# Expert slots with one and two turns between their stages, four slots' rows transposed together, all three expert weights copied by ScalarE, and the slot row numbers worked out right behind the tables

## The reference

```python
x = x + L0_attn(layernorm(x))      # 16 sequences of 512 tokens, 128 features: time mixing with a scan, then channel mixing
x = x + L0_ffn(layernorm(x))       # 8192 tokens, 16 experts, the best one alone (K = 1)

logits = hidden @ router_w.T                              # [8192, 16]
top_vals, top_idx = top_k(logits, 1)
scores = sigmoid(scatter(top_vals, at top_idx, else -inf))
routed_in = hidden[None] * scores.T[:, :, None]           # a token's row, scaled, in its own expert; zero in the others
gate, up = split(routed_in @ gate_up_proj[e])             # 128 -> 2 x 128
routed_out = (up * silu(gate)) @ down_proj[e]             # 128 -> 128
shared = silu(hidden @ shared_gate.T) * (hidden @ shared_up.T) @ shared_down.T    # 128 -> 512 -> 128, for every token
return shared + sum over experts of routed_out
```

## Time and profile before

| | us |
|---|---|
| median of the runs | 578.75 |
| the profiled execution, its own time | 577.51 |
| its span, first to last instruction | 575.7 |

### The profile page before, as it was taken

The page is one execution under the profiler, slowest core; times in us unless marked ns, Lnnn a source line. Parts: engine busy times, 40 slices in busy tenths (PEclk is TensorE's granted clock), DMA queues, the critical chain, the costliest instruction groups (busy, mean ns, idle before and its releaser), DMA issues.

```text
span 575.7 us, 10804 instructions
## 1 busy us (share of the span) xinstructions
PE 498.0 (86%) x3012; PEld 401.3 (70%) x3012; DVE 386.0 (67%) x1075; ACT 325.9 (57%) x619; POOL 353.1 (61%) x548
## 2 busy tenths in 40 slices
PE   1778999999999999999999999996698888888730
PEld 0346777877868877878768777995488777777730
DVE  3769999989999799988999797363132233322213
ACT  3666886767876776857776753421154445535410
POOL 5445478768778578867878466447026565565560
PEclk9888999999999999999999999997699999999965
DMA  6005101101101011101011011106423443344207
GB/s 201 1 1 209 49 1 56 57 1 57 38 19 55 12 47 56 37 21 56 10 47 38 2 38 37 38 29 156 112 83 111 112 119 112 111 116 121 77 3 219
DMA packets 34923, 38.30 MB, mean 67 GB/s; under 512 B 4946, under 2 KB 30938, under 8 KB 34609
## 3 DMA queue, kind: packets, MB, share of 16 engines
q1 hardware_dynamic: 25680, 22.61, 13.5%
q0 software_dynamic: 5920, 13.42, 6.9%
q10 hardware_dynamic: 3264, 1.57, 0.9%
HBM read 21.15 MB, written 17.47 MB: 67 GB/s over the span
## 4 chain that ended last, share of the span: by engine, by line
PE 59%; DVE 12%; issue 10%; POOL 7%; ACT 6%; another core or an unknown queue 3%; DMA 1%; POOLq 0%; SPq 0%; DVEq 0%; ACTq 0%
PE bank L344 14%; PE bank L353 9%; PE bank L337 6%; PE bank L608 4%; DVE an L811 3%; PE bank L331 3%; PE bank L601 2%; PE bank L380 2%; PE bank L602 2%; PE bank L397 2%; PE bank L420 2%; PE bank L384 2%; PE bank L433 2%; PE bank L413 2%
## 5 line engine op out<-in xcount | busy, mean ns | idle before, releaser
L344 PE MATMUL bank<-hT,wm 128*128 128x256 f32 x512 | 125.6, 390 | 3.8 <-issue 3.1
L1155 POOL DMA_INDIRECT out<-shared x80 | 78.7, 983 | 78.8 <-DVE shared L1012 56.6
L344 PEld LDWEIGHTS bank<-hT,wm 128*128 128x128 f32 x512 | 95.5, 194 | 22.9 <-issue 11.1
L1012 DVE TENSOR_TENSOR shared<-bank,shared 128x256 f32<-128x256 f32 x40 | 17.0, 425 | 78.4 <-remote 54.7
L337 PE MATMUL bank<-wm,k 128*128 128x128 f32 x512 | 63.9, 279 | 2.8 <-ACT k L650 2.8
L337 PEld LDWEIGHTS bank<-wm,k 128*128 128x128 f32 x512 | 62.4, 196 | 4.4 <-ACT k L650 3.6
L608 PE MATMUL bank<-wdn,e 128*128 x160 | 29.9, 310 | 17.5 <-DVE e L1017 15.1
L811 DVE TENSOR_SCALAR an<-a,mvC,smC 128x128 f32<-128x128 f32 x64 | 43.2, 735 | 1.4 <-POOL smC L1059 1.4
L608 PEld LDWEIGHTS bank<-wdn,e 128*128 128x128 f32 x160 | 23.1, 196 | 22.8 <-issue 22.1
L601 PE MATMUL bank<-num,q 128*128 128x128 f32 x160 | 31.7, 280 | 6.4 <-ACT num L757 5.6
L353 PEld LDWEIGHTS bank<-wm,actA 128*128 128x128 f32 x240 | 30.2, 192 | 6.7 <-issue 6.7
(11 more groups left out here) (187 smaller groups left out, 1288.2 us busy)
## 6 DMA issues: line engine op xcount, KB each, us to landing
shared<-sorted_rows SPq DMA_DIRECT2D x80, 128.5 KB
shared<-x SPq DMA_DIRECT2D x16, 256.0 KB
wgu<-w_gu SPq DMA_DIRECT2D x1, 2048.0 KB, 8.4
sorted_rows<-filler SPq DMA_DIRECT2D x11, 128.5 KB
out<-shared POOLq DMA_INDIRECT x80
wdn<-w_down SPq DMA_DIRECT2D x1, 1024.0 KB, 10.3
sorted_rows<-rows,posi POOLq DMA_INDIRECT x64
wm<-w_main SPq DMA_DIRECT2D x1, 776.0 KB, 7.4
```

What stands on the lines that cost most here:

```text
L344: ins = mm(dst[:, j * HALF:(j + 1) * HALF], W(name, 2 * pair_ + j), src[:, half * HALF:(half + 1) * HALF], start=True, stop=True)
L1155: g_.indirect_dma_start(out, bass.IndirectOffsetOnAxis(xr[k % RING][:, j, 2 * D:ROW].bitcast(U32), 0), xr[k % RING][:, j, D:2 * D], None, ...
```

## The change

1. The transposes of two pairs (four slots) are made in the even turns, into one bank (bank 6), and DVE copies them with one instruction of 128x512 (`xhT4`), where ACT made one copy of 128x256 a pair. The even pair's gate and up products follow one turn later, the odd pair's two turns later.
2. ACT copies gate, up and down weights of a slot with one instruction of 128x384 out of `wexp`, into five pairs of buffers (it waits for the down product of five pairs before). PE's down product has no register address any more, and PE doesn't read `eid_i`.
3. Down products alternate between banks 5 and 1, so PE waits for `xy` of two pairs before; `xact` has four buffers.
4. `row_i` and `eid_i` are worked out in `tables`, right behind the table's other numbers, with DVE waiting there for PE's two small matmuls. ACT reads `eid_i` in the last round, ahead of its copy of the last `C_TILES` unit.
5. PE's wait for that copy stands ahead of unit 3's first down product, not ahead of unit 3. The late steps are interleaved: unit u+1's first step comes before unit u's down products. Still eight ahead of the slots (now five gate and up, three down), still 28 in the turns, from turn 1 on.
6. A late unit's two groups of tokens are the even and the odd rows of the unit (`unit_down_late` reads its stationary operand with a step of two numbers), so in the last read and write of `out` each partition has 1024 bytes in one piece where it had two of 512.
7. In a row the token's number stands between input and base, not at the end. Some waits that stood beside each other changed places.

```diff
-        xhT, xsg, xact = ([b[:, i * 2 * P:(i + 1) * 2 * P] for i in range(2)] for b in (num[0], num[1], e[0]))
-        xw = q
+        xhT4, xsg, xact = [*num, er[1]], halves(er[0]), halves(*e)
+        def xhT(k, j):
+            return grp(xhT4[k // 2 % 3], 2 * (k % 2) + j)
+        xw = [q, an, xn2T, th, rv]
+        XW = len(xw)
-        XT6_B, XGU_B, XDN_B = [bank[6], bank[1]], [bank[4], bank[7]], bank[5]
+        XT6_B, XGU_B, XDN_B = bank[6], [bank[4], bank[7]], [bank[5], bank[1]]
-            return rows[t % 3][:, :, D:2 * D]
+            return rows[t % 3][:, :, D + 1:ROW]
...
+        def late_order():
+            order = [(FIRST_LATE, 0), (FIRST_LATE, 1)]
+            for u in range(FIRST_LATE + 1, N_LATE):
+                order += [(u, 0), (u - 1, 2), (u, 1), (u - 1, 3)]
+            return order + [(N_LATE - 1, 2), (N_LATE - 1, 3)]
         def late_steps(m):
-            n_steps = 4 * (N_LATE - BEFORE_SLOTS)
-            return [(BEFORE_SLOTS + i // 4, i % 4) for i in range(n_steps) if 2 + i * (NP - 4) // n_steps == m]
+            steps = late_order()[STEPS_BEFORE:]
+            return [step for i, step in enumerate(steps) if LATE_TURN + i * (NP - 2) // len(steps) == m]
...
-                return out[row:row + HALF, :].rearrange("(g p) d -> p g d", p=P)
+                return out[row:row + HALF, :].rearrange("(p g) d -> p (g d)", g=2)
...
+            def unit_down_late(acc, lhs, pair_):
+                for j in range(2):
+                    for g in range(2):
+                        ins = mm(grp(acc, g), lhs[:, j * HALF + g:(j + 1) * HALF:2], W("down", 2 * pair_ + j),
+                                 start=(pair_ == 0 and j == 0 and g == 0), stop=(pair_ == 1 and j == 1), skip_group_check=True)
+                return ins
...
                 else:
+                    if u == FIRST_LATE:
+                        wait(pe, "cbase", NT)
                     wait(pe, "lac", u, step - 1)
...
-            wait(pe, "cbase", NT)
-            late_step(FIRST_LATE, 0)
-            late_step(FIRST_LATE, 1)
-            pe.wait_ge(s["tab"], TAB_ROWS + 2)
-            words = list(entries(PE_ENGINE, eid_i, 0, NE ** PACK - 1, WORDS))
-            late_step(FIRST_LATE, 2)
-            late_step(FIRST_LATE, 3)
-            for u in range(FIRST_LATE + 1, BEFORE_SLOTS):
-                for step in range(4):
-                    late_step(u, step)
-            pe.wait_ge(s["w_in3"], 32)
+            for u, step in late_order()[:STEPS_BEFORE]:
+                late_step(u, step)
             def one_turn(m):
-                for k in pair(m, 0):
-                    pe.wait_ge(s[f"xr_in{k % RING}"], 32 * (k // RING + 1))
-                    wait(pe, "xhT", k - 2)
-                    for j in range(2):
-                        ins = nc.tensor.transpose(grp(XT6_B[k % 2], j), xr[k % RING][:, j, 0:D], ident[:, :])
+                for k in two_pairs(m):
+                    wait(pe, "xhT", k // 2 - 1)
+                    for i in range(4):
+                        if i % 2 == 0:
+                            pe.wait_ge(s[f"xr_in{(k + i // 2) % RING}"], 32 * (k // RING + 1))
+                        ins = nc.tensor.transpose(grp(XT6_B, i), xr[(k + i // 2) % RING][:, i % 2, 0:D], ident[:, :])
                     ins.then_inc(s["xT6"], 1)
...
                 for k in pair(m, 2):
                     wait(pe, "xact", k)
-                    wait(pe, "xy", k - 1)
+                    wait(pe, "xy", k - 2)
                     for j in range(2):
-                        ins = mm(grp(XDN_B, j), grp(xact[k % 2], j), wdn[:, bass.ds(expert_of(words, 2 * k + j) * D, D)], start=True, stop=True)
+                        ins = mm(grp(XDN_B[k % 2], j), grp(xact[k % 4], j), w_of(k, j, 2), start=True, stop=True)
...
# ScalarE
+                    if t == C_TILES[-1]:
+                        load_words()
                     wait(act_e, "cD1", t)
...
-                    wait(act_e, "xGU", k - 2)
+                    wait(act_e, "xDN", k - XW)
                     for j in range(2):
-                        af(xw[k % 2][:, j * 2 * EF:(j + 1) * 2 * EF],
-                           wgu[:, bass.ds(expert_of(words, 2 * k + j) * (2 * EF), 2 * EF)], ACT.Copy).then_inc(s["xw"], 1)
-                    wait(act_e, "xT6", k)
-                    af(xhT[k % 2][:, :], XT6_B[k % 2][:, 0:2 * P], ACT.Copy).then_inc(s["xhT"], 1)
+                        af(xw[k % XW][j][:, 0:EW], wexp[:, bass.ds(expert_of(words, 2 * k + j) * EW, EW)], ACT.Copy).then_inc(
+                            s["xw"], 1)
...
# VectorE
                 assert ntab[0] == TAB_ROWS
+                dve.wait_ge(s["tab_mm"], 1)
+                tab(v.tensor_scalar(row_i[0:1, :], TAB[0:1, 0:NS], float(P), None, ALU.mult))
+                tab(v.tensor_copy(eid_i[0:1, :], TAB[0:1, P:P + WORDS]))
...
             def one_turn(m):
+                for k in two_pairs(m):
+                    wait(dve, "xT6", k // 2)
+                    wait(dve, "xGU", k - 5)
+                    v.tensor_copy(xhT4[k // 2 % 3][:, :], XT6_B[:, :]).then_inc(s["xhT"], 1)
```

More of the change, by code:

```diff
@@ L297, in _ @@
                 if t == XR:
-                    sp.dma_start(wgu[:, :], w_gu).then_inc(s["w_in3"], 16)
-                    sp.dma_start(wdn[:, :], w_down).then_inc(s["w_in3"], 16)
+                    for n in range(2):
+                        part = slice(n * NE // 2 * EW, (n + 1) * NE // 2 * EW)
+                        sp.dma_start(wexp[:, part], w_exp[:, part]).then_inc(s["w_in3"], 16)
             sp.wait_ge(s["tab"], 1)
@@ L622, in _, with load_words @@
             act_e.wait_ge(s["const_p"], 6)
+            words = []
+            def load_words():
+                act_e.wait_ge(s["tab"], TAB_ROWS + 2)
+                words.extend(entries(ACT_ENGINE, eid_i, 0, NE ** PACK - 1, WORDS))
             def one_round(n):
```

83 lines of the change are left out of this document (38 added, 45 removed).

## The result

The changed kernel takes 576.0 us, the median of five runs (575.05 to 576.62), against 578.65 for the kernel before in as many (577.65 to 579.56). The ratio is 0.9953, with a 95% interval of 0.9936 to 0.997: 2.65 us faster. The time lies in the forecast's range and has its sign. The size is wrong: 8.75 us were forecast and under a third of it came. The nearest case is the rival "the slots stay as they are" (575.3).

A forecast was written before the change was run, and what follows sets the result against it. PE's completions, seen late during POOL's scatter runs, bound the slots. Gains of 2.4 (ahead), 5.3 (slots) and 1.0 (end), 8.7 us, take 577.51 to 568.8; the median's 1.24 more makes 570.0, range 559 to 581.5.

The forecast's parts named there:

- the slots stay as they are: Rival: in the slots POOL's lock keeps 3.335 us a pair, only 3.4 us are won, 575.3 us; 13%.
- What bounds the slots: In the slots no engine is full; PE's completions come late during POOL's scatter runs, 3.335 us a pair.
- The slots' pace, 3.20: In the slots a third pair gets into POOL's runs more often: 3.20 us a pair, 5.3 us won.
- Ahead of the slots: PE's late steps before the first transposes end at 417.2 instead of 421.35: 4.2 us, of which 2.4 reach POOL.
- the cover: In the last round ACT's 8.66 idle us hide its reading of the words, at most 6.1 us: no cost.
- From transposes to addition: From the first transpose to the first addition: 6.4 us, where it was 4.64.
- The end: Last read and write of the output, with pieces of 1024 bytes: 1.0 us won.
- Stepped operand: PE's late down products read their stationary operand with a step of two: no cost, loads stay at 0.19 us.
- DVE's copies beside POOL: In the slots DVE's 20 copies of 0.69 us don't hold up POOL's scatters; otherwise up to 13.8 us.
- PE gets full: Rival: in the slots PE works through POOL's runs, 2.72 us a pair, 551.3 us; 13%.
- The lock gets worse: Rival: in the slots four transposes keep every third pair out of POOL's runs, 3.49 us a pair, 581.3 us; 10%.
- the stepped loads cost: Rival: doubled stationary loads in PE's late down products, half of 23 us visible, 582 us; 3%.

The follow-up runs named there:

- the pause: The changed kernel with POOL zeroing 128x512 numbers ahead of each pair's two scatters: 570.0 us, ratio 0.9854; on another chip, with all fills on SP too, 559.0 us.

## Why the prediction was wrong

**What bounds the slots: right.** PE's late signals during POOL's runs set the pace on a late chip. Where they come in time the kernel before is 31 us faster, 27.0 of it in the scatters (106.5 us for 133.5) and 3.9 from the tables to the first one; with the late steps taken away it stays at 3.17 a pair. What isn't shown is why a chip delays them, nor whether it always does: each was seen for one group of runs. Whether the recording of the trace has a part in it wasn't tested either. On a late chip ACT's register operations are slowed too under POOL's fills (11.0 us for the words, 5.1 without the fills, 5.2 with them on a timely chip), so it is not a matter of PE alone.

**The slots' pace, 3.20: the step that failed.** I wrote that three pairs with one restart take "6 x 0.98 + 5 x 0.30 + 2.13 = 9.51, 3.17 a pair", and that more sixes would come. They came: six runs of six and one of ten, where before there was one above five. But 2.13 is the restart after a four. After a run of six the changed kernel's POOL stands still for 2.55 us in the mean (2.22 to 3.04), and with the 7.44 that the six take, 10.0 for three pairs are 3.33 a pair, not 3.17. Six such restarts are 2.5 us over the forecast's, of the 3.0 by which the scatters' stretch misses it (131.2 against 133.5 - 5.3 = 128.2). The end of one such run:

```profile
489.26 0.61 PE L630 MATMUL bank<-rv,e 128*128 128x128 f32 x4
489.50 0.98 POOL L1178 DMA_INDIRECT out<-shared  x1 [0.30 <-issue]
491.72 0.69 DVE L1023 TENSOR_TENSOR actB<-sgB,bank 128x512 f32<-128x512 f32 x1 [4.12 <-issue]
492.32 0.42 DVE L1035 TENSOR_TENSOR shared<-bank,shared 128x256 f32<-128x256 f32 x1
493.53 0.98 POOL L1178 DMA_INDIRECT out<-shared  x1 [3.04 <-DVE shared L1035]
```

The first signal comes at 491.64, 1.15 us after the run's end (1.1 to 1.2 in four of the six, 0.9 in the other two, and 0.8 to 0.9 after a four). Then a late product (0.60) that waited for the same burst goes ahead of the addition, and 1.2 pass from the addition to the scatter. Another restart (2.71) has the new copy of 128x512 in that place.

By its own measure, the additions, the forecast's pace came nearly: 428.07 to 554.34 us are 3.24 a pair in place of 3.335, 3.8 us of the 5.3. But the sum let the kernel end with the last addition. POOL had a last run of ten scatters to do, and from the last addition to the last scatter's end it was 6.2 us where it had been 4.7. That leaves 2.3 of the 5.3.

**Ahead of the slots: the place was right, the cover wasn't; the second step that failed.** PE's 4.2 us went. The forecast gave ACT's reading at most 6.1 us and called it nothing, since PE needs ACT's copy only for a down product. It overlooked that ACT's first late Silu stands behind the reading too, and that PE needs it for the next gate and up step. The 6.1 held on timely chips (5.2) and with the fills on SP (5.1), not under POOL's run of fills on the late chip, where the reading took 11.0 and PE stalled 6.32. The low clock behind the stall took 2.3 us more (two steps in 6.26 us; 3.96 with the fills on SP). So the first transposes won 2.2 us in place of 4.2 (25.7 behind the tables, 27.8 before), and 0.7 reached POOL in place of 2.4. On a timely chip they won 4.7 (19.3 for 24.0), but PE then waits 1.57 us for the rows, a bound to which I had given no price, and the clock sometimes falls behind that wait. That the one trace shown there has just the forecast's 2.4 is luck.

**From transposes to addition:** forecast 6.4, measured 428.07 - 421.99 = 6.1 on the late chip, at the full clock.

**The end:** forecast 1.0, measured 1.5 and 1.1, of which part 6 is 0.8.

**Stepped operand:** nothing forecast, 4 ns a load measured. The Trainium skill (SBUF — State Buffer, Door 1: The DMA port swizzle) says that accesses run at full rate as long as two of them fall in one 16-byte line, and the trace agrees within 2% (196 ns against 192).

**DVE's copies beside POOL:** 0.69 us each, and the 18 scatters that run beside one still take 984 ns in the mean, as forecast. The Trainium skill (VectorE: DVE Perf Modes, Why PSUM operands drop a tier) says that an operand in PSUM keeps DVE out of the mode that takes both SBUF read ports, and the trace agrees with what the forecast took from it: no scatter is lengthened.

**The rivals.** "PE gets full" was wrong on both kinds of chip: on timely ones it is POOL that gets full, at 2.6. "The slots stay" came nearest in time, by luck: the pace of the additions did move, by 0.1 us a pair. "The lock gets worse" and "the stepped loads cost" were wrong.

## What to carry to other kernels

A wait that ends "remote", with a producer long done, can be a signal on its way; a stage bound by it gained little from deeper rings here (2.3 us of 133; what tight rings do on a late chip wasn't measured), and what stands ahead of the waited-for instruction when the burst comes counts more. Take the length of a restart for each length of run from the trace, not one for all. Follow what is moved to another engine down that engine's list: here the reading of the words was cheap for the instruction that was looked at, and dear for the next one. Measure on more than one chip before a remedy is kept: the pause that gave 6 us on one cost 16 on another, while the change itself gained on both kinds (2.65 and 4.7 us).

## What the runs showed of the hardware

- The same program took 579.2 us on one chip and 547 to 548 on three others; from 82 us to the tables both kinds took the same time, within 1 us (311.8 and 311.0 us), and the difference lies where POOL issues indirect DMAs back to back.
- On the late chip PE's semaphore updates then come one at a time, some 0.7 or 1.5 us apart, and in a burst that begins 0.8 to 1.2 us after the end of a run of DMA_INDIRECT (491.64, 491.73, 491.79, 491.88, 491.94, 1.15 to 1.45 after it); during POOL's run of fills register operations of ACT take 0.70 us there, and 0.15 otherwise and on a timely chip.
- POOL's memsets took 246, 352 and 565 ns for 128, 256 and 512 columns.
- The moment at which PE's granted clock reaches its full level in the first 40 us differs from run to run: between the two shown traces 2.7 us hang on it.
- The same gate and up step took 1.89 us at a granted clock of 1.00 and 3.53 at 0.50, in two traces whose programs are the same up to there, after waits of PE of 1.57 and 0.55 us in one and 1.52 and 0.84 in the other.
